# A gated cross-attention and sparse feed-forward kernel: a reordered attention loop, the context's first loads on ScalarE's queue, and moved splits in the feed-forward

## The chip, the core and the metric

The kernel runs on one core of one Trainium2 chip. The metric is the device time of one execution in microseconds (us); less is better. A core has TensorE (PE, with PEld for its weight loads), VectorE (DVE), ScalarE (ACT), GpSimd (POOL) and SyncE (SP), each with its own instruction stream; they meet in semaphores. 16 DMA engines move data between HBM and the on-chip SBUF.

## What is computed

The inputs are x [32, 128, 512], a context of the same shape, a mask [32, 128], two scalar gates and three weights of the feed-forward (512 by 2048 twice, 2048 by 512). `_layernorm` is (x - mean) / sqrt(var + 1e-5). Cut to what matters:

```python
q = _layernorm(x)
scores = einsum('bsd,bmd->bsm', q, ctx) / sqrt(512)
attn = softmax(where(mask[:, None, :], scores, -1e30))
out = einsum('bsm,bmd->bsd', attn, ctx)
out = where(any(mask, -1)[:, None, None], out, 0)
x = x + tanh(g_xattn[0]) * out

n = _layernorm(x)
h = silu(n @ w_gate) * (n @ w_up)
# in each group of 4 neighbours of h the 2 of largest magnitude are kept
x = x + tanh(g_ffn[0]) * (sparsify_2to4(h) @ w_down)
```

## The kernel before

**Attention.** A loop over 39 slots (n from 0 to 38; DVE and POOL start one or two earlier) is software-pipelined over 32 batches of one 128 by 512 tile. Each engine has its own copy of the loop, written out by hand, and in slot n works on several batches at once. On DVE slot n holds two `bn_aggr` (statistics of batch n-6's new row tile and of batch n+1's input; results in `bn_mv`), `neg_scores` and its minimum `neg_max` (batch n-3), `x1`, the attention's output plus x (n-5), `x1n`, that tile normalised (n-6), and two `bn_stats`, of `x1` (n-5) and of `x_in` (n+2). POOL turns variances into powers: `base3` adds eps, `power3` raises to -0.5 (and the softmax sum to -1), `neg_mean` and `neg_mean_rstd` make the bias of `xn`. ACT copies transposed tiles out of PSUM (`ctxT`, `xnT`), makes `probs` (exp), `xn` and `probsT`. PE transposes and multiplies. SP issues the loads, nine batches ahead (INPUTS = 9), and the stores.

**The first weights and activations.** The feed-forward multiplies in float32r with a high and a low part for each operand, and replaces eight block products by seven (PROD = 7) of sums of blocks. Tables by slot place this preparation in the attention loop: `PIECE_AT` (loads of raw weights), `SPREAD_AT` (ACT copies a raw piece into `w_blk`), `SUM_AT` (DVE sums of blocks), `W0_AT` and `X0_AT` (ACT makes the high part, POOL the low part one slot later: `w_ring`, L306, and `xm`, L347; DVE makes the sums of `x_blk` at L354 to L364). A DVE `w_sum` or `x_sum` stands between `neg_max` and `x1`.

**Feed-forward.** 16 steps s of two units u = 2s and 2s+1. A unit is seven products k (two halves e each, 12 matmuls of 128 x 512 per k) followed, from u = 2 on, by the down product of four row tiles (`ps_y`, 48 matmuls). PE starts the first three products in slots 36 to 38. Product 2 waits until ACT has copied product 0 out (`copy_a0`), product 5 for `copy_d0`, a row tile for `copy_y` (`y_out`) of the tile two before it. While weights are built (u < 8) and while the next pair's activations are split (14 points, `x_point(s, point)`), ACT makes `x_high` and DVE `x_low` (L347, `x_out`) and then the next `x_sum`. `dn_low` (L1020) makes the low part of w_down.

What the change and the prediction touch: the start of SP's queue (L421 to L430), the DVE slot (L888 to L943), POOL's slot (L520 to L552), the tables, and the places of `x_high_at`, `x_low_at`, `spread` and `dn_low` in ACT's and DVE's feed-forward code.

Of the kernel before, what the change touches and what calls it, by code (L numbers as in the profile page):

```python
# [5 lines left out]
F32 = mybir.dt.float32  # L6
# [24 lines left out]
BIG = 1e30  # L31
RING = 8
# [15 lines left out]
CONVERT = {1: (0,), 2: (1,), 3: (2, 3)}  # L48
# [6 lines left out]
PIECE_AT = {4: (0, 2), 7: (0, 3), 10: (1, 0), 13: (1, 1), 21: (1, 2), 24: (1, 3), 27: (2, 0), 30: (2, 1)}  # L55
SPREAD_AT = {3: (0, 0), 6: (0, 1), 9: (0, 2), 12: (0, 3), 20: (1, 0), 23: (1, 1), 26: (1, 2), 29: (1, 3)}
SUM_AT = {13: ((0, 0), (0, 1)), 14: ((0, 2),), 15: ((0, 3),), 30: ((1, 0), (1, 1))}
W0_AT = {5: 0, 8: 1, 14: 2, 15: 3, 16: 4, 17: 5, 18: 6}
X0_AT = {19 + i: (0, i) for i in range(7)} | {29 + i: (1, i) for i in range(7)}
# [41 lines left out]
def flamingo_gated(nc, x, ctx, mask, g_xattn, g_ffn, w_gate, w_up, w_down, out):  # L101
# [9 lines left out]
    with whole:  # L111
# [36 lines left out]
        neg_scores = sb("neg_scores", [P, 2, M], F32, 4)  # L148
# [9 lines left out]
        bn_mv = sb("bn_mv", [P, RING, 2, 2], F32, 4)  # L158
# [5 lines left out]
        eps = sb("eps", [P, 2], F32, 4)  # L164
# [3 lines left out]
        valid = sb("valid", [P, B], F32, 4)  # L168
        gate_valid = sb("gate_valid", [P, B], F32, 4)
        ident = sb("ident", [P, P], F32, 4)  # L170
        x_blk1 = sb("x_blk1", [P, 4, HALF], F32, 4)
        mask_in = x1nT[:, 0, 0:2].rearrange("p c n -> p (c n)").bitcast(U8)

# [202 lines left out]
        def _(sp):  # L376
            def load(b):
# [3 lines left out]
                sp.dma_start(ctx_in[:, b % INPUTS], ctx[b]).then_inc(ctx_in_loaded[b % INPUTS], 16)  # L381
# [38 lines left out]

            for b in range(INPUTS):  # L421
                load(b)
                if b == 1:
                    sp.dma_start(mask_in, mask.rearrange("b m -> (b m)").rearrange("(a n) -> a n", a=1)
                                 .to_broadcast([P, B * M])).then_inc(mask_loaded, 16)
# [3 lines left out]
            load_w_piece(sp, nc.sync, 0, 0)  # L429
            load_w_piece(sp, nc.sync, 0, 1)  # L430
# [162 lines left out]
        def _(act):  # L593
# [5 lines left out]
            for n in range(SLOTS):  # L599
# [736 lines left out]
```

## Time and profile before

| | |
|---|---|
| median of 3 runs | 1119.65 us (1117.45 to 1120.14) |
| the profiled execution: its own time | 1116.94 us |
| its span (first to last instruction) | 1115.1 us |
| PE / DVE / ACT / POOL busy, share of the span | 97% / 73% / 56% / 19% |
| granted TensorE clock, mean | 0.998 |
| attention ends, first feed-forward product begins | 134.58 us |

Times in the trace are us from the start of the span. A row of the timeline is start, duration, engine, line, operation, tile written and tiles read, shapes, and, in brackets, how long the engine had been idle and what released it. SPq is SP's DMA issue; its duration is that of the issue, not of the transfer. Time outside the span is 1.8 us.

### The profile page before, as it was taken

Reading aid. Unit: us, or ns where it says so; the run is one execution under the profiler, and the core shown is the slowest. Engines: PE = TensorE matmul, PEld = TensorE weight load, DVE = VectorE, ACT = ScalarE, POOL = GpSimd, SP = SyncE. Lnnn points to the kernel's source line nnn. Section 1 sums busy time; section 2 is a strip of 40 time slices with the busy share of each in tenths; the row PEclk is TensorE's granted clock in tenths of the full one; section 3 lists DMA queues with packets and bytes.
Section 4 is the critical chain, followed back from the end, with each engine's and each line's share of the span. In section 5 each row is a group of like instructions: output and inputs, shape, how many; then the busy total and the mean of one; then the engine's idle time right before and its main releaser. Section 6 shows DMA issues by size and latency. Waiting matters only on the chain.

```text
span 1115.1 us, 15146 instructions
## 1 busy us (share of the span) xinstructions
PE 1082.4 (97%) x4960; PEld 880.0 (79%) x4960; DVE 809.6 (73%) x1400; ACT 620.1 (56%) x1132; POOL 210.6 (19%) x328
## 2 busy tenths in 40 slices
PE   6998799999999999999999999999999999999998
PEld 5776587777878888888888888888888888888886
DVE  6999969879897757576775767675757565565765
ACT  5999678566765544454544444454445454443452
POOL 5576610121210111111111111001111111111111
PEclk9999999999999999999999999999999999999999
DMA  7899586798869977797779777888878666767726
GB/s 273 295 349 329 202 326 226 219 289 280 257 226 354 356 196 198 187 257 185 202 197 374 182 202 200 237 235 208 231 230 274 151 153 156 189 159 189 199 29 137
DMA packets 89533, 254.75 MB, mean 228 GB/s; under 512 B 9072, under 2 KB 9072, under 8 KB 85104
## 3 DMA queue, kind: packets, MB, share of 16 engines
q1 hardware_dynamic: 67856, 205.55, 52.2%
q0 software_dynamic: 21600, 48.24, 26.1%
q8 instruction: 40, 0.66, 0.2%
q14 instruction: 37, 0.30, 0.1%
HBM read 154.14 MB, written 99.61 MB: 228 GB/s over the span
## 4 chain that ended last, share of the span: by engine, by line
PE 73%; DVE 14%; ACT 4%; issue 4%; POOL 2%; DMA 2%; SPq 0%; DVEq 0%; ACTq 0%; POOLq 0%
PE ps_y L1302 9%; PE ps_a L1231 9%; PE ps_a L1233 9%; PE ps_a L1235 9%; PE ps_y L1304 9%; PE ps_y L1303 9%; PE ps_d L1233 4%; PE ps_d L1231 4%; PE ps_d L1235 4%; PE ps_c L1233 2%; PE ps_c L1231 2%; PE ps_c L1235 2%; DVE beats L980 2%; DMA w_raw<-in_L_ffn_w_up 1%; DVE x1n L930 1%
## 5 line engine op out<-in xcount | busy, mean ns | idle before, releaser
L569 POOL DMA_DIRECT2D out_rows<-y_out x124 | 107.1, 871 | 735.2 <-ACT y_out L717 712.7
L1231 PE MATMUL ps_a<-xm,w_ring 128*128 128x512 f32 x512 | 200.7, 392 | 3.6 <-ACT cp L597 3.3
L1233 PE MATMUL ps_a<-xm,w_ring 128*128 128x512 f32 x512 | 200.3, 391 | 0.0
L1235 PE MATMUL ps_a<-xm,w_ring 128*128 128x512 f32 x512 | 200.2, 391 | 0.0
L1302 PE MATMUL ps_y<-dn,h_hi 128*128 128x512 f32 x480 | 188.9, 394 | 4.4 <-ACT y_out L717 3.3
L1304 PE MATMUL ps_y<-dn,h_lo 128*128 128x512 f32 x480 | 187.4, 390 | 0.0
L1303 PE MATMUL ps_y<-dn,h_hi 128*128 128x512 f32 x480 | 187.0, 390 | 0.0
L717 ACT ACTIVATE y_out<-ps_y,ffn_gate 128x512 f32<-128x512 f32 x124 | 84.8, 686 | 158.4 <-PE ps_y L1304 158.3
L694 ACT ACTIVATE h_hi<-hidden 128x512 fp32r<-128x512 f32 x128 | 73.6, 626 | 107.0 <-DVE hidden L1006 107.0
L980 DVE TENSOR_TENSOR beats<-h_abs 128x512 bf16<-128x512 f32 x186 | 117.7, 684 | 1.3 <-ACT h_abs L687 1.3
L1231 PEld LDWEIGHTS ps_a<-xm,w_ring 128*128 128x128 f32 x512 | 96.4, 188 | 26.2 <-issue 5.2
L1235 PEld LDWEIGHTS ps_a<-xm,w_ring 128*128 128x128 f32 x512 | 96.5, 188 | 20.4
L1233 PEld LDWEIGHTS ps_a<-xm,w_ring 128*128 128x128 f32 x512 | 96.4, 188 | 20.0
L1302 PEld LDWEIGHTS ps_y<-dn,h_hi 128*128 128x128 f32 x480 | 90.1, 188 | 27.4 <-ACT y_out L717 7.4
L948 DVE TENSOR_TENSOR cp<-ps_c,cp 128x512 f32<-128x512 f32 x64 | 43.6, 689 | 93.7 <-PE ps_c L1235 93.7
L1304 PEld LDWEIGHTS ps_y<-dn,h_lo 128*128 128x128 f32 x480 | 90.1, 188 | 19.4
L1303 PEld LDWEIGHTS ps_y<-dn,h_hi 128*128 128x128 f32 x480 | 90.2, 188 | 18.7
L1231 PE MATMUL ps_d<-xm,w_ring 128*128 128x512 f32 x256 | 99.7, 390 | 0.5 <-ACT hidden L670 0.5
L1235 PE MATMUL ps_d<-xm,w_ring 128*128 128x512 f32 x256 | 99.6, 389 | 0.0
L1233 PE MATMUL ps_d<-xm,w_ring 128*128 128x512 f32 x256 | 99.6, 389 | 0.0
L954 DVE TENSOR_TENSOR hidden<-ps_a,hidden 128x512 f32<-128x512 f32 x64 | 43.8, 690 | 65.2 <-PE ps_a L1235 62.9
L687 ACT ACTIVATE h_abs<-hidden 128x512 f32<-128x512 f32 x124 | 74.1, 625 | 28.3 <-DVE hidden L972 28.3
(109 smaller groups left out, 1876.6 us busy)
## 6 DMA issues: line engine op xcount, KB each, us to landing
w_ring<-w_scratch SPq DMA_DIRECT2D x147, 512.0 KB, 4.5
out_rows<-y_out POOLq DMA_DIRECT2D x124, 256.0 KB, 4.3
w_scratch<-w_ring SPq DMA_DIRECT2D x56, 512.0 KB, 4.7
xm_scratch<-x_out SPq DMA_DIRECT2D x42, 512.0 KB, 5.4
xm<-xm_scratch SPq DMA_DIRECT2D x21, 1024.0 KB, 8.4
w_raw<-in_L_ffn_w_down SPq DMA_DIRECT2D x9, 1024.0 KB, 7.8
x_in<-in_x SPq DMA_DIRECT2D x32, 256.0 KB, 4.7
ctx_in<-in_ctx SPq DMA_DIRECT2D x32, 256.0 KB, 5.0
```

The lines of the kernel that those rows point to most:

```text
L569: nc.gpsimd.dma_start(out[RING * (n // (2 * TILES * QS)) + TILES * ORDER[order] + n % TILES], y_out[:, n % 4], accum_op=ALU.add).then_inc( ...
L687: nc.scalar.activation(abs_of(s, order)[:, j], hidden[:, h, j], ACT.Abs).then_inc(abs_done, 1)
L694: nc.scalar.activation(h_hi[:, h, j], hidden[:, h, j], ACT.Copy).then_inc(h_hi_done, 1)
L717: nc.scalar.activation(y_out[:, n % 4], ps_y[n % 2][:], ACT.Identity, scale=ffn_gate[:]).then_inc(y_copied, 1)
L954: nc.vector.tensor_tensor(hidden[:, 1, j], ps_a[e][:], hidden[:, 1, j], ALU.add).then_inc(c22_done[e], 1)
L980: nc.vector.tensor_tensor(beats[:, PAIR[i, j]], abs_of(s, order)[:, i], abs_of(s, order)[:, j], ALU.is_ge).then_inc(beats_done, 1)
L1231: nc.tensor.matmul(to, w_ring[:, k, e, 0, c], xm[:, k, 0, c], start=begins and c == 0, stop=False, skip_group_check=not begins)
L1233: nc.tensor.matmul(to, w_ring[:, k, e, 0, c], xm[:, k, 1, c], start=False, stop=False, skip_group_check=not begins)
L1235: last = nc.tensor.matmul(to, w_ring[:, k, e, 1, c], xm[:, k, 0, c], start=False, stop=c == 1, skip_group_check=not begins)
L1302: nc.tensor.matmul(to, h_hi[:, h, j, at], right[:, 0, j], start=at_j == 0, stop=False)
L1303: nc.tensor.matmul(to, h_hi[:, h, j, at], right[:, 1, j], start=False, stop=False)
L1304: last = nc.tensor.matmul(to, h_lo[:, h, j, at], right[:, 0, j], start=False, stop=at_j == GROUP - 1)
```

## The change

- **Context loads.** ACT issues the loads of `ctx_in` 0 to 8 before its loop; SP issues the others.
- **Mask.** One load of 128 x 4096 bytes becomes four of 128 x 1024, and the four reductions `valid` and the product `gate_valid` go. `neg_scores` gets a 129th column of 0.9e30, so that a fully masked batch has all its probabilities 0; `LEAST` keeps the sum of them above 0.
- **POOL.** The softmax sum now lies in `stats` (formerly `bn_mv`) with the variances; one `base3` add covers all and so waits for `probs` too. `neg_mean` moves ahead of `power3`.
- **DVE slot.** `bn_stats` of `x_in` moves from the slot's end to just behind `x1`, ahead of `x1n`. `x_sum` is made in the slot of `X0_AT`, formerly one slot earlier.
- **Tables.** Weight pieces 2 and 3 are loaded, spread and summed earlier, sums one in a slot; the second half of the first pair's activations is split in slots 26 to 32, formerly 29 to 35.
- **Feed-forward.** `x_high_at(s, 3)` and `x_low_at(s, 3)` move into the next step, `x_high_at(s, 1)` behind the next `copy_a0`, `spread(u + 1, 2)` behind `silu1`, `dn_low` ahead of two compares.

```diff
-CONVERT = {1: (0,), 2: (1,), 3: (2, 3)}
+CONVERT = {1: 0, 5: 1, 7: 2, 10: 3}
-W0_AT = {5: 0, 8: 1, 14: 2, 15: 3, 16: 4, 17: 5, 18: 6}
-X0_AT = {19 + i: (0, i) for i in range(7)} | {29 + i: (1, i) for i in range(7)}
+W0_AT = {5: 0, 8: 1, 12: 2, 13: 3, 14: 4, 15: 5, 16: 6}
+X0_AT = {19 + i: (0, i) for i in range(7)} | {26 + i: (1, i) for i in range(7)}
...
         def _(sp):
             def load(b):
...
-                sp.dma_start(ctx_in[:, b % INPUTS], ctx[b]).then_inc(ctx_in_loaded[b % INPUTS], 16)
+                if b >= INPUTS:
+                    sp.dma_start(ctx_in[:, b % INPUTS], ctx[b]).then_inc(ctx_in_loaded[b % INPUTS], 16)
...
             for b in range(INPUTS):
                 load(b)
...
+                if b == 5:
+                    load_w_piece(sp, nc.sync, 0, 0)
+                    load_w_piece(sp, nc.sync, 0, 1)
+                if b == 7:
+                    load_mask(1)
+                if b == 2:
+                    load_mask(0)
...
         def _(pool):
...
                 if third:
                     pool.wait_ge(probs_done, n - 3)
-                part_p = slice(0 if first else 1, 3 if third else 2 if second else 1)
+                nc.gpsimd.tensor_tensor(base3[:, k, part_p], stats[:, k, part_p, 1], least[:, part_p],
+                                        ALU.add).then_inc(base_done, 1)
+                if first:
+                    nc.gpsimd.tensor_tensor(neg_mean[:, k:k + 1], stats[:, k, 0, 0:1], minus_one[:],
+                                            ALU.mult).then_inc(neg_mean_done, 1)
+                pool.wait_ge(base_done, n + 2)
                 nc.gpsimd.tensor_tensor(power3[:, k, part_p], base3[:, k, part_p], exponent3[:, part_p],
                                         ALU.pow).then_inc(power_done, 1)
...
         def _(act):
...
+            for b in range(INPUTS):
+                act.dma_start(ctx_in[:, b], ctx[b]).then_inc(ctx_in_loaded[b], 16)
             for n in range(SLOTS):
...
                     absolute(s - 1, 1, 1)
                     copy_a0(u, 1)
+                    x_high_at(s - 1, 3)
...
-                    x_high_at(s, 1)
...
                     w_high(act, 2, 6)
-                    x_high_at(0, 3)
                     continue
...
                 copy_a0(u, 1)
+                x_high_at(s, 1)
...
                     w_high(act, u + 1, 0)
-                    spread(act, u + 1, 2)
                 silu1(u, 0)
                 silu1(u, 1)
                 if building:
+                    spread(act, u + 1, 2)
                     w_high(act, u + 1, 1)
                     spread(act, u + 1, 3)
...
         def _(dve):
...
-                    dve.wait_ge(mask_loaded, 16)
-                    for m in CONVERT[n]:
-                        nc.vector.tensor_reduce(valid[:, m * RING:(m + 1) * RING],
...
                 if s > 1:
                     add_c11(u, 0)
                     add_c11(u, 1)
+                    x_low_at(s - 1, 3)
...
-                    x_low_at(s, 0)
                     add_c22(u, 0)
                     add_c22(u, 1)
-                    compare(s - 1, 1, REST[2:])
                     if s - 1 in DN_BUILT:
                         dn_low(s - 1)
+                    x_low_at(s, 0)
+                    compare(s - 1, 1, REST[2:])
...
                 elif s == 1:
                     for j in tiles:
                         h_low(0, 0, j)
+                    x_low_at(0, 3)
```

The order of DVE's instructions in one slot with a sum, before (slot 22; names as in the text above, `x_65` is `x1`, `bn_68` the raw statistics):

```order
L892 BN_AGGR bn_mv<-bn_68 128x2
L896 BN_AGGR bn_mv<-bn_68 128x2
L909 SCALAR_TENSOR_TENSOR neg_scores<-ps_c,mask_neg 128x128
L912 TENSOR_REDUCE neg_max<-neg_scores 128x1
L357 TENSOR_TENSOR x_blk<-x_blk 128x512
L924 SCALAR_TENSOR_TENSOR x_65<-ps_y,power_71,x_in 128x512
L930 TENSOR_SCALAR x1n<-x_65,bn_mv,power_71 128x512
L935 BN_STATS bn_68<-x_65 128x6
L943 BN_STATS bn_68<-x_in 128x6
```

and in the changed kernel such a slot on DVE reads:

```order
L903 BN_AGGR stats<-bn_68 128x2
L907 BN_AGGR stats<-bn_68 128x2
L914 SCALAR_TENSOR_TENSOR neg_scores<-ps_c,mask_neg 128x128
L919 TENSOR_REDUCE neg_max<-neg_scores 128x1
L361 TENSOR_TENSOR x_blk<-x_blk 128x512
L930 SCALAR_TENSOR_TENSOR x_65<-ps_y,power_71,x_in 128x512
L935 BN_STATS bn_68<-x_in 128x6
L940 TENSOR_SCALAR x1n<-x_65,stats,power_71 128x512
L945 BN_STATS bn_68<-x_65 128x6
```

The statistics of `x_in` have moved from behind the other two to ahead of `x1n`.

DVE in the first step with a down product (s = 1, unit 2), before; `hidden` is what is kept, `beats` a compare:

```order
L1006 SCALAR_TENSOR_TENSOR hidden<-part,hidden 128x512
L347 TENSOR_TENSOR x_out<-x_blk,x_out 128x512
L357 TENSOR_TENSOR x_blk<-x_blk 128x512
L1013 TENSOR_TENSOR h_lo<-hidden,h_hi 128x512 x4
```

and in the changed kernel at the same place on DVE:

```order
L1008 SCALAR_TENSOR_TENSOR hidden<-part,hidden 128x512
L1015 TENSOR_TENSOR h_lo<-hidden,h_hi 128x512 x4
L351 TENSOR_TENSOR x_out<-x_blk,x_out 128x512
L361 TENSOR_TENSOR x_blk<-x_blk 128x512
L982 TENSOR_TENSOR beats<-h_abs 128x512 x2
```

The low part of the activations and the sum behind it now follow the four `h_lo`.

## Rows read from the trace of the kernel before

**Rows 1.** The stretch behind the build, by windows: length, busy time (instructions).
```profile
340.00:1080.00 740.00, 740.00 (x3253) 609.69 (x3252) 490.20 (x802) 356.22 (x617) 83.89 (x98) 1.00 0.78 213
```

**Rows 2.** Timeline of the start, ACT, DVE; and SP's line L381.
```profile
0.72 1.28 ACT L617 ACT_TABLE_LOAD   x1 [0.72 <-PEq L1326]
5.89 0.81 ACT L617 ACTIVATE xn<-x_in,neg_mean_rstd,power 128x512 f32<-128x512 f32 x1 [3.88 <-POOL neg_mean_rstd L542]
10.48 0.69 DVE L943 BATCH_NORM_STATS2 bn<-x_in 128x6 f32<-128x512 f32 x1 [3.37 <-DMA x_in<-in_x]
15.15 2.31 DVE L900 TENSOR_REDUCE valid<-x1nT 128x8 f32<-128x1024 uint8 x2
26.33 0.75 DVE L924 SCALAR_TENSOR_TENSOR x<-ps_y,power,x_in 128x512 f32<-128x512 f32 x1 [0.26 <-PE ps_y L1272]
...
L381 SPq DMA_DIRECT2D ctx_in<-in_ctx x32: 418/450/1503, 1.2 to 105.4; - x32
```

**Rows 3.** Timeline of one attention slot without a low part on POOL.
```profile
35.11 0.17 DVE L892 BATCH_NORM_AGGREGATE bn_mv<-bn 128x2 f32<-128x6 f32 x1
35.77 0.85 POOL L535 TENSOR_TENSOR power<-base,exponent 128x3 f32<-128x3 f32 x1
36.72 0.55 DVE L930 TENSOR_SCALAR x1n<-x,bn_mv,power 128x512 f32<-128x512 f32 x1
38.38 0.17 DVE L892 BATCH_NORM_AGGREGATE bn_mv<-bn 128x2 f32<-128x6 f32 x1
```

**Rows 4.** Timeline of slot 21, with a sum and a low part.
```profile
78.60 0.16 DVE L892 BATCH_NORM_AGGREGATE bn_mv<-bn 128x2 f32<-128x6 f32 x1
79.32 0.68 DVE L354 TENSOR_TENSOR x_blk<-x_blk 128x512 f32<-128x512 f32 x1
79.92 0.75 DVE L924 SCALAR_TENSOR_TENSOR x<-ps_y,power,x_in 128x512 f32<-128x512 f32 x1
80.07 0.19 POOL L538 TENSOR_TENSOR neg_mean<-bn_mv,minus_one 128x1 f32<-128x1 f32 x1
80.48 1.27 POOL L347 TENSOR_TENSOR xm<-x_blk,xm 128x512 fp32r<-128x512 f32 x1
80.58 1.45 DVE L930 TENSOR_SCALAR x1n<-x,bn_mv,power 128x512 f32<-128x512 f32 x1
83.15 0.16 DVE L892 BATCH_NORM_AGGREGATE bn_mv<-bn 128x2 f32<-128x6 f32 x1
```

**Rows 5.** Timeline of slot 20, with a low part and no sum.
```profile
76.94 0.55 DVE L930 TENSOR_SCALAR x1n<-x,bn_mv,power 128x512 f32<-128x512 f32 x1
77.49 1.27 POOL L347 TENSOR_TENSOR xm<-x_blk,xm 128x512 fp32r<-128x512 f32 x1
```

**Rows 6.** Timeline of slots 34 and 35, the end of attention.
```profile
127.99 0.18 DVE L892 BATCH_NORM_AGGREGATE bn_mv<-bn 128x2 f32<-128x6 f32 x1
132.70 1.41 DVE L930 TENSOR_SCALAR x1n<-x,bn_mv,power 128x512 f32<-128x512 f32 x1 [0.46 <-POOL power L535]
```

**Rows 7.** Timeline of the first pair: TensorE's waits and what stands ahead.
```profile
181.27 0.47 PE L1231 MATMUL ps_a<-xm,w_ring 128*128 128x512 f32 x1 [1.91 <-ACT cp L597]
190.64 0.63 ACT L342 ACTIVATE x_out<-x_blk 128x512 fp32r<-128x512 f32 x1 [0.57 <-DVE x_blk L357]
192.04 0.47 PE L1231 MATMUL ps_d<-xm,w_ring 128*128 128x512 f32 x1 [0.54 <-ACT hidden L670]
...
216.32 0.47 PE L1231 MATMUL ps_a<-xm,w_ring 128*128 128x512 f32 x1 [1.35 <-ACT cp L597]
...
231.02 1.12 ACT L290 ACTIVATE w_blk<-w_raw 128x512 f32<-128x512 f32 x1 [5.04 <-DMA w_raw<-in_L_ffn_w_up]
237.51 0.50 PE L1302 MATMUL ps_y<-dn,h_hi 128*128 128x512 f32 x1 [1.84 <-ACT y_out L717]
...
294.60 0.69 DVE L972 TENSOR_TENSOR hidden<-hidden,cp 128x512 f32<-128x512 f32 x1 [2.03 <-ACT cp L678]
324.93 0.50 PE L1302 MATMUL ps_y<-dn,h_hi 128*128 128x512 f32 x1 [1.09 <-DVE dn L1020]
```

More of the change, by code:

```diff
@@ L31 @@
 BIG = 1e30
+FEW = 0.9e30
+LEAST = 1e-30
 RING = 8
@@ L163, in flamingo_gated @@
         neg_mean_rstd = sb("neg_mean_rstd", [P, RING], F32, 4)
-        eps = sb("eps", [P, 2], F32, 4)
+        least = sb("least", [P, 3], F32, 4)
         minus_one = sb("minus_one", [P, 1], F32, 4)
@@ L526, in _ @@
                     pool.wait_ge(stats2_done, n - 5)
-                if first or second:
-                    part_v = slice(0 if first else 1, 2 if second else 1)
-                    nc.gpsimd.tensor_tensor(base3[:, k, part_v], bn_mv[:, k, part_v, 1], eps[:, part_v],
-                                            ALU.add).then_inc(base_done, 1)
-                    pool.wait_ge(base_done, n + 2)
+                part_p = slice(0 if first else 1, 3 if third else 2 if second else 1)
                 if third:
                     pool.wait_ge(probs_done, n - 3)
-                part_p = slice(0 if first else 1, 3 if third else 2 if second else 1)
+                nc.gpsimd.tensor_tensor(base3[:, k, part_p], stats[:, k, part_p, 1], least[:, part_p],
[4 more added lines that the diff above has]
+                pool.wait_ge(base_done, n + 2)
                 nc.gpsimd.tensor_tensor(power3[:, k, part_p], base3[:, k, part_p], exponent3[:, part_p],
@@ L544, in _ @@
                 if n in CONVERT:
[L545 to L549 removed]
+                    m = CONVERT[n]
+                    pool.wait_ge(mask_loaded[m], 16)
+                    part_m = slice(m * GROUP_M, (m + 1) * GROUP_M)
+                    nc.gpsimd.tensor_scalar(mask_neg[:, part_m], mask_in[:, part_m], -BIG, BIG, ALU.mult,
+                                            ALU.add).then_inc(mask_neg_done, 1)
                 if n - 1 in W0_AT:
@@ L610, in _ @@
                     wait(act, pT_done, b - 1)
-                    nc.scalar.activation(probs[:, b % 2], neg_scores[:, b % 2], ACT.Exp, bias=neg_max[:, b % RING:b % RING + 1],
-                                         scale=-1.0, accum_out=base3[:, (b + 4) % RING, 2:3]).then_inc(probs_done, 1)
+                    nc.scalar.activation(probs[:, b % 2], neg_scores[:, b % 2, 0:M], ACT.Exp, bias=neg_max[:, b % RING:b % RING + 1],
+                                         scale=-1.0, accum_out=stats[:, (b + 4) % RING, 2, 1:2]).then_inc(probs_done, 1)
                 b = n
@@ L914, in _ @@
                 if n in SUM_AT:
-                    for u, i in SUM_AT[n]:
-                        w_sum(dve, u, i)
-                if n + 1 in X0_AT:
-                    x_sum(dve, 0, *X0_AT[n + 1])
+                    w_sum(dve, *SUM_AT[n])
+                if n in X0_AT:
+                    x_sum(dve, 0, *X0_AT[n])
                 b = n - 5
@@ L925, in _ @@
                                                    x_in[:, b % INPUTS], ALU.mult, ALU.add).then_inc(x1_done, 1)
+                b = n + 2
+                if b < B:
+                    dve.wait_ge(x_in_loaded[b % INPUTS], 16 * (b // INPUTS + 1))
+                    nc.vector.bn_stats(bn6[:, 0, b % 2], x_in[:, b % INPUTS]).then_inc(bn1_done, 1)
                 b = n - 6
```

95 lines of the change are left out of this document (37 added, 58 removed).

## The prediction, made before the changed kernel was run

> **What bounds the kernel now.** I read the windows first. From 340 us on TensorE is busy for the whole of each window, 740 of 740 us, while VectorE has a third of its time free [rows 1]. Nothing that the change does there can gain, and it adds no work to TensorE. What can gain is the attention phase (to 134.6 us) and TensorE's waits while weights are built (135 to 340 us). Second, the timeline of the start. VectorE sits 3.37 us until the third x tile lands, then makes the four mask reductions, and ScalarE has its first work only at 5.89 us [rows 2]. Third, the timeline of single slots: VectorE goes from one slot into the next with hardly an idle gap, so that the length of its slot sets the pace [rows 3 to 5]. Fourth, the list of TensorE's waits in the first pair [rows 7].
>
> **The slot of VectorE, which carries the sum.** A slot without a low part on GpSimd takes 38.38 - 35.11 = 3.27 us [rows 3]. In it x1n starts 1.61 us after the slot's first row, though VectorE could reach it at 1.38 (1.98 in slot 21 [rows 4], less 0.60 for the sum ahead of it: 79.92 - 79.32). It waits for power, 35.77 + 0.85 = 36.62. The change puts bn_stats of x_in (0.60: x1n and two of them take 38.38 - 36.72 = 1.66, and x1n 0.46) into this gap: minus 0.23. But the slot's first bn_aggr now reads what the instruction just ahead of it made; I add 0.10 for the 0.69 of its full length in place of the 0.60 from start to start. New free slot: 3.27 - 0.23 + 0.10 = about 3.15.
>
> A slot with a low part is another matter. In slot 20 x1n starts at 76.94 and the low part follows at 77.49, just when x1n ends [rows 5]. In slot 21 the low part starts first, at 80.48, and x1n, issued at 80.58, takes 1.45 in place of 0.55: it ends at 82.03, which is 0.28 behind the end of the low part, 80.48 + 1.27 = 81.75 [rows 4]. The slot is 83.15 - 78.60 = 4.55 long. So whoever starts first makes the other wait. Measured from the slot's first row the low part starts at 1.88 and x1n at 1.98 with a sum; without one x1n came first. After the change x1n starts 0.60 later in each slot, at 1.98 without a sum and 2.58 with one. The low part starts a little earlier than 1.88, since neg_mean (80.07, between power and the low part) goes ahead of power; I take 1.74. It wins in every slot. The new slot is 1.74 + 1.27 + 0.28 = 3.29 to the end of x1n, minus 0.08 of overlap, plus 0.71 for the last bn_stats: 3.92, with or without a sum, against 3.27 and 4.55.
>
> The Trainium skill says the same of the mechanism and speaks against the change (SBUF — State Buffer, "SBUF: two separate sides"): VectorE and GpSimd share a port pair, an exclusive lock for the whole instruction, and the one that starts first gets it. By this rule the trace agrees (1.45 against 0.55).
>
> **Attention, term by term.** I count from x1 in slot 6 to x1n in slot 35, which releases TensorE's transposition and the first product. Before: 132.70 - 26.33 = 106.4 us. After: low parts lie in slots 6, 9, 13 to 17 and 20 to 30, 18 slots, and I count the mask conversions in slots 7 and 10 like them: 20 x 3.92 = 78.4. Slots 8, 18 and 19 are free: 3 x 3.15 = 9.5. Slots 11 and 12 have a sum alone: 2 x 3.75 = 7.5. Slots 31 to 33, which have no bn_stats of x_in any more, stay at the 3.4 of now (slot 34 too: 132.70 - 127.99, less 1.33 to x1n [rows 6]), 10.2. Slots 34 and 35 up to x1n took 132.70 - 127.99 = 4.7 with low parts [rows 6]; without them power, 0.5 behind the slot's first row and 0.8 long, sets about 1.3 in each and x1n and bn_stats follow: 3.8. Sum 109.4, less 0.72, at which x1 stands in its slot (79.92 - 78.60 less the sum's 0.60): 108.7, that is 2.3 slower. In this sum the low parts of 30 to 36 that now end in slot 33, and the stall and double sums of slot 13, are already gained; the collisions take more than all of it. At the end x1n itself has no collision and takes 0.55, not 1.41 [rows 6]: minus 0.9.
>
> **The start.** The third x tile no longer stands behind the whole mask and three context tiles: its 3.37 us go. The reductions go from VectorE, 2 x 2.31 = 4.6 us for four. But ScalarE must first issue nine loads. No row shows a load issued by ScalarE. SP's take 0.42 at least, 1.50 at most [rows 2]. From below: 0.73 + 9 x 0.42 + 1.28 for the table load (which now stands behind them) = 5.8, no later than now. From above: 0.73 + 9 x 1.50 + 1.28 = 15.5. I take 0.6 each, nearer the lower end, as SP's median is 0.45, with something for the second queue that fills beside it; so 7.4, 1.5 late. Then each slot is a round through ScalarE and TensorE, some 2.6 us at first, 3.3 with probs, and about 3.5 in slots 3 and 4, each of which now holds a spread. I get xn of slot 4 at about 19.5 and x1 of slot 6 some 3.6 behind it, 23.1 to 23.3, where 26.33 stands now: minus 3.2. The rest of the 8.0 us removed is lost to that round.
>
> The Trainium skill's DMA page (DMA: Bandwidth & Descriptors, "Issuing engines are not separate DMA queues") says that issuing from several engines only saves issue time. No run here shows more; it would leave the bytes' time as it is.
>
> Attention together: 2.3 - 0.9 - 3.2 = -1.8 us.
>
> **The first pair.** (1) The wait of 1.91 at 181.27 goes: ScalarE stood at x_high of point 3, behind VectorE's sum, and the copy behind it was late; the copy now comes first. (2) What is late next: ScalarE's x_high of step 1 waits for the sum of that same point (190.64 [rows 7]), which VectorE now makes behind four h_lo, 4 x 0.60 = 2.4 us later. Behind it in ScalarE's queue stand the two copy_d0, for which product 5 waits. It starts 2.4 later, at 192.04 + 2.4 = 194.4 (times of before). TensorE, there at 192.04 - 0.54 - 1.91 = 189.6, waits 4.8 in place of 0.54. (3) The wait of 1.35 at 216.32 absorbs most of this: 4.8 against 1.91 + 0.54 + 1.35 = 3.8. Net +1.0 at most. (4) At 237.51 the chain hangs on a weight piece that lands at 231.02; with x_high(1, 1) out of the way ScalarE frees its buffer some 0.9 earlier: net -0.9 there, as TensorE waits 1.84 at that place and the +1.0 is absorbed in it. (5) silu1 no longer stands behind the spread that waits for a load, so VectorE's 2.03 at 294.60 shrink, and dn_low comes 1.2 to 2.4 earlier: of the wait of 1.09 at 324.93 and what VectorE, which is full there, holds up beside it I take 1.3, between 0 and the 2.03. Sum: -2.2 us; bounds +0.5 (4 and 5 bring nothing) and -4.
>
> **Sum.** -1.8 - 2.2 = -4.0. The profiled execution took 1116.94, so 1112.9; its time is 2.7 below the median of the three, and from the median it is 1119.65 - 4.0 = 1115.6. That is 0.36% faster, just past the 0.3% (3.4 us) that a measurement of this kernel can tell from no change.
>
> **Rivals.** (A) The low part does not win the race. Speaking for it: the margin without a sum is 1.98 - 1.74 = 0.24 us, and base3 now also waits for probs. Against it: 0.10 was enough in slot 21. Then 11 slots without a sum (6, 13 to 17, 20, 21, 26 to 28) fall to about 3.3, ScalarE's own slot: 11 x 0.6 = 6.6 more, 1109.
>
> (B) Slower than before: ScalarE's nine issues clog. Its queue backs up as SP's did at its worst (1.50). At 1.5 each xn starts at 15.5, 8.1 later than I take: 1115.6 + 8.1 = 1123.7. Equality with before lies at 0.6 + 4.0/9 = 1.04 us per issue. For it: ScalarE does nothing else meanwhile, all later work hangs on it, and it has eight loads queued at its ninth. Against it: SP's median is 0.45. The Trainium skill (Perfetto Trace Analysis, "DMA Instruction — HWDGE (DVE, Sync)") says that a load's descriptors come from a generator that one sequencer locks at a time; no row here has two sequencers at it. By that rule each issue would wait for one of SP's, 2 x 0.45 = 0.9, xn would start at 10.1, and the sum would be 2.7 less, 1118.3.
>
> (C) The first pair gives nothing, or the 4.8 us wait is not absorbed: -1.8 + 0.5 to +2.5, so 1118 to 1120, within 0.3%. For it: VectorE is full in that stretch and each delay moves on.
>
> (D) The loads don't arrive earlier: DMA engines carry the same bytes, and the third x tile lands only when six tiles are through. For it: the volume is unchanged, and the context's share now flows beside x from the first tile on. Then the start keeps 1 of its 3.2: 1117.8.
>
> **How the numbers follow.** Forecast, between -7 and -1.5 us, 0.50; A 0.12; B 0.14; C 0.14; D 0.10. Predicted time 1115.6. The range 1108.5 to 1121.5 takes in A at its foot and B up to 1.3 us an issue. Faster by over 0.3%: A, and 0.44 of the forecast and rest, 0.58; within 0.3% 0.26; slower 0.16.
>
> **What would show it.** ScalarE's first xn between 6 and 9 us; x1 of slot 6 near 23; x1n taking 1.3 to 1.5 us in nearly all of the slots with a low part, and these 3.9 long; the first product near 132.3. In unit 2 one wait of TensorE for copy_d0 of 4 to 5 us where there were two small ones, and no wait before product 2. It is wrong if x1n stays at 0.55 in slots without a sum, if the nine issues take over 9 us, or if TensorE waits anywhere behind 340 us.

## The result and the profile after

The changed kernel takes 1129.06 us (median; 1125.18 to 1132.69) against 1119.65 in the same runs: a ratio of 1.0082, 95% interval 1.0055 to 1.0109. It is slower by about 9 us. The prediction was 1115.6 us, with a range that ended at 1121.5 and 0.16 on slower. The profiled execution took 1129.06 us with a span of 1127.3, so that 1.8 us lie outside the span, as before.

The first view is again the windows: the stretch behind the build, in which TensorE was busy for every one of 740 us [rows 1].

```profile
340.00:1080.00 740.00, 729.14 (x3192) 599.40 (x3191) 480.21 (x785) 346.67 (x604) 83.26 (x97) 1.00 0.77 212
```

TensorE is idle for 10.9 us there, and does 61 matmuls fewer (3192 for 3253). The timeline of TensorE has these waits in it, those of the first pair ahead of them (which answer to [rows 7]; a further one of 0.58 at 268.16, like the 0.58 before, is left out):

```profile
181.63 0.47 PE L1233 MATMUL ps_a<-xm,w_ring 128*128 128x512 f32 x1 [0.77 <-ACT cp L675]
190.37 0.76 PE L1233 MATMUL ps_d<-xm,w_ring 128*128 128x512 f32 x1 [5.78 <-ACT hidden L681]
235.67 0.50 PE L1304 MATMUL ps_y<-dn,h_hi 128*128 128x512 f32 x1 [1.92 <-ACT y_out L728]
329.64 0.50 PE L1304 MATMUL ps_y<-dn,h_hi 128*128 128x512 f32 x1 [1.17 <-ACT y_out L728]
382.58 0.55 PE L1233 MATMUL ps_d<-xm,w_ring 128*128 128x512 f32 x1 [3.59 <-ACT hidden L681]
516.77 0.50 PE L1304 MATMUL ps_y<-dn,h_hi 128*128 128x512 f32 x1 [1.43 <-ACT y_out L728]
578.53 0.50 PE L1304 MATMUL ps_y<-dn,h_hi 128*128 128x512 f32 x1 [1.46 <-ACT y_out L728]
639.43 0.50 PE L1304 MATMUL ps_y<-dn,h_hi 128*128 128x512 f32 x1 [0.59 <-ACT y_out L728]
761.13 0.50 PE L1304 MATMUL ps_y<-dn,h_hi 128*128 128x512 f32 x1 [1.46 <-ACT y_out L728]
823.77 0.50 PE L1304 MATMUL ps_y<-dn,h_hi 128*128 128x512 f32 x1 [2.33 <-ACT y_out L728]
1101.31 0.48 PE L1304 MATMUL ps_y<-dn_last,h_hi 128*128 128x512 f32 x1 [1.09 <-DVE h_lo L1015]
```

The last row, the first of the last down products, stands in both kernels. The kernel before has it, and the row tile that answers to 329.64, here:

```profile
331.30 0.50 PE L1302 MATMUL ps_y<-dn,h_hi 128*128 128x512 f32 x1 [0.59 <-ACT y_out L717]
1089.21 0.47 PE L1302 MATMUL ps_y<-dn_last,h_hi 128*128 128x512 f32 x1 [1.09 <-DVE h_lo L1013]
```

So two numbers say where the time went. I call these two rows the first and the last mark. At the first mark the changed kernel is 331.30 - 329.64 = 1.66 us ahead. From the first to the last mark it takes 771.67 us where the kernel before took 757.91: 13.8 more. I call this stretch the tail; it is the measure of the experiments below. Of the 13.8, 10.9 are the six waits. Another 1.7 are 3.4 us behind the wait at 382.58 in which the granted clock stood at 1.2 GHz (from 382.8 on; before, the clock was at 1.00 for all of this stretch). The last 1.2 I could not place in a single row.

The wait at 382.58 is read on ScalarE: `x_high` stands 7.13 us for x_blk (2.64 before), and `copy_d0` (L681), which TensorE needs, stands behind it. SP shows why x_blk is late:

```profile
344.01 1.09 SPq L392 DMA_DIRECT2D xm_scratch<-x_out  x1
350.48 4.40 SPq L423 DMA_DIRECT2D xm<-xm_scratch  x7
354.99 0.58 SPq L283 DMA_DIRECT2D x_blk<-xnT_scratch  x1
381.32 0.63 ACT L346 ACTIVATE x_out<-x_blk 128x512 fp32r<-128x512 f32 x1 [7.13 <-DMA x_blk<-xnT_scratch]
381.86 1.06 ACT L681 ACTIVATE hidden<-ps_d 128x512 f32<-128x512 f32 x2
```

The seven loads of xm read what the stores of x_out have written, so SP waits for the last store to land: issued at 344.01, it leaves a hole of 5.3 us in SP's queue. Before, the hole was 0.5 us. The load of x_blk itself is not issued late: 354.99 here and 356.57 before. What the hole costs is the time of the DMA engines, which have little to do in it, so that the 7 MB of xm, and x_blk behind them, are carried later. x_blk takes 26.3 us from issue to landing where it took 21.9. The windows of the changed kernel (the last two numbers are the share of the DMA engines and GB/s):

```profile
348.00:350.00 2.00, 2.00 (x11) 1.65 (x10) 1.07 (x2) 0.00 (x0) 0.00 (x0) 1.00 0.46 169
350.00:352.00 2.00, 2.00 (x10) 1.68 (x9) 0.92 (x2) 0.63 (x1) 0.00 (x0) 1.00 0.43 70
```

and of the kernel before:

```profile
348.00:350.00 2.00, 2.00 (x10) 1.68 (x9) 0.74 (x2) 0.58 (x1) 0.00 (x0) 1.00 1.03 416
350.00:352.00 2.00, 2.00 (x10) 1.65 (x10) 0.72 (x2) 0.00 (x0) 0.00 (x0) 1.00 1.03 356
```

The waits for y_out have another origin. In the list of waits, `dn_high` on ScalarE now waits for the down weights:

```profile
ACT dn L718 <- DMA w_raw<-in_L_ffn_w_down: 11.4, 4, 3.2
```

that is 11.4 us in 4 waits, none of which was there before. The load stands on SP directly behind a store of x_out and is issued at 498.25, where the kernel before issued it at 489.73. The store waits for the low part that the change moved into the next step (`x_out`, 496.91 to 497.59; it was made at 488.39):

```profile
497.62 0.53 SPq L392 DMA_DIRECT2D xm_scratch<-x_out  x1
498.25 0.55 SPq L415 DMA_DIRECT2D w_raw<-in_L_ffn_w_down  x1
```

In the attention phase the timeline shows the start (it answers to [rows 2]) and the slots ([rows 3 to 6]):

```profile
0.72 5.60 ACTq L610 DMA_DIRECT2D ctx_in<-in_ctx  x9
7.65 0.81 ACT L629 ACTIVATE xn<-x_in,neg_mean_rstd,power 128x512 f32<-128x512 f32 x1
12.57 0.69 DVE L935 BATCH_NORM_STATS2 bn<-x_in 128x6 f32<-128x512 f32 x1 [4.25 <-DMA x_in<-in_x]
22.86 0.74 DVE L930 SCALAR_TENSOR_TENSOR x<-ps_y,power,x_in 128x512 f32<-128x512 f32 x1
48.34 1.27 POOL L310 TENSOR_TENSOR w_ring<-w_blk,w_ring 128x512 fp32r<-128x512 f32 x1
48.50 1.40 DVE L940 TENSOR_SCALAR x1n<-x,stats,power 128x512 f32<-128x512 f32 x1
52.46 1.39 DVE L940 TENSOR_SCALAR x1n<-x,stats,power 128x512 f32<-128x512 f32 x1
82.55 1.27 POOL L351 TENSOR_TENSOR xm<-x_blk,xm 128x512 fp32r<-128x512 f32 x1
83.33 0.77 DVE L940 TENSOR_SCALAR x1n<-x,stats,power 128x512 f32<-128x512 f32 x1
129.65 0.55 DVE L940 TENSOR_SCALAR x1n<-x,stats,power 128x512 f32<-128x512 f32 x1 [0.47 <-POOL power L547]
130.66 0.48 PE L1233 MATMUL ps_a<-xm,w_ring 128*128 128x512 f32 x1
```

The row at 129.65 is x1n of the batch that [rows 6] show at 132.70: it starts 3.05 us earlier, and takes 0.55 in place of 1.41. The last row is the first feed-forward product, which stood at 134.58: attention ends 3.92 us earlier. A low part on GpSimd and x1n end 0.28 or 0.29 us apart both without a sum (49.61 and 49.90) and with one (83.82 and 84.10).

### The profile page after: what moved, and what is told of

Read it like the earlier page. It is cut to its first block, busy times and chain, and to the rows that moved or that the text cites. A ratio compares the mean times of both kernels' runs of the same rounds, so it can differ in the third digit from the quotient of the medians.

```text
span 1127.3 us, 15122 instructions
## 1 busy us (share of the span) xinstructions
PE 1084.2 (96%) x4960; PEld 880.3 (78%) x4960; DVE 806.8 (72%) x1395; ACT 617.2 (55%) x1132; POOL 205.9 (18%) x330
## 4 chain that ended last, share of the span: by engine, by line
PE 67%; DVE 16%; DMA 7%; ACT 5%; issue 4%; ACTq 1%; SPq 0%; POOL 0%; DVEq 0%
PE ps_y L1304 8%; PE ps_y L1306 8%; PE ps_y L1305 8%; PE ps_a L1233 8%; PE ps_a L1237 8%; PE ps_a L1235 8%; PE ps_d L1233 4%; PE ps_d L1235 4%; PE ps_d L1237 4%; DMA w_raw<-in_L_ffn_w_down 2%; DMA x_blk<-xnT_scratch 2%; PE ps_c L1237 2%; PE ps_c L1233 2%; PE ps_c L1235 2%; DVE x1n L940 2%
## 5 line engine op out<-in xcount | busy, mean ns | idle before, releaser
L1304 PE MATMUL ps_y<-dn,h_hi 128*128 128x512 f32 x480 | 189.0, 394 | 10.9 <-ACT y_out L728 10.9
L1233 PE MATMUL ps_d<-xm,w_ring 128*128 128x512 f32 x256 | 101.3, 396 | 9.4 <-ACT hidden L681 9.4
L1235 PE MATMUL ps_d<-xm,w_ring 128*128 128x512 f32 x256 | 101.2, 395 | 0.0
L1237 PE MATMUL ps_d<-xm,w_ring 128*128 128x512 f32 x256 | 101.0, 394 | 0.0
```

Source lines behind the costliest of these rows:

```text
L1233: nc.tensor.matmul(to, w_ring[:, k, e, 0, c], xm[:, k, 0, c], start=begins and c == 0, stop=False, skip_group_check=not begins)
L1235: nc.tensor.matmul(to, w_ring[:, k, e, 0, c], xm[:, k, 1, c], start=False, stop=False, skip_group_check=not begins)
L1237: last = nc.tensor.matmul(to, w_ring[:, k, e, 1, c], xm[:, k, 0, c], start=False, stop=c == 1, skip_group_check=not begins)
L1304: nc.tensor.matmul(to, h_hi[:, h, j, at], right[:, 0, j], start=at_j == 0, stop=False)
```

## The experiments

The programs, and for each the start of the first mark, the length of the tail, the time of the profiled execution from which these two are read, and the median of all executions. The kernel before was timed again beside runs 1 to 4, 5 to 8 and 9 to 12; its median there was 1118.41, 1118.99 and 1119.28, so ratios are the better comparison. A mark comes from one execution, which can lie up to 2.7 us above or below its median (the kernel before is 2.7 below, run 5 is 1.7 above, run 10 is 1.2 below, run 8 is 2.5 above).

| kernel | first mark | tail | profiled | median | ratio to before (95%) |
|---|---|---|---|---|---|
| before | 331.30 | 757.91 | 1116.94 | 1119.65 | |
| changed | 329.64 | 771.67 | 1129.06 | 1129.06 | 1.0082 (1.0055 to 1.0109) |
| 1 attention alone | 330.39 | 757.92 | 1116.03 | 1116.08 | 0.9971 (0.9960 to 0.9982) |
| 2 feed-forward alone | 331.40 | 769.63 | 1128.73 | 1130.89 | 1.0109 (1.0092 to 1.0127) |
| 3 three mends | 327.13 | 764.63 | 1119.50 | 1119.66 | 1.0011 (1.0000 to 1.0023) |
| 4 down weights first | 327.62 | 766.88 | 1122.25 | 1123.22 | 1.0044 (1.0027 to 1.0061) |
| 5 four mends | 328.29 | 759.23 | 1115.25 | 1113.51 | 0.9948 (0.9935 to 0.9961) |
| 6 five mends | 327.10 | 760.52 | 1115.36 | 1114.70 | 0.9959 (0.9947 to 0.9971) |
| 7 attention, context on SP | 327.15 | 760.03 | 1115.28 | 1114.75 | 0.9962 (0.9950 to 0.9974) |
| 8 before, one store moved | 336.62 | 764.87 | 1129.25 | 1126.76 | 1.0071 (1.0059 to 1.0084) |
| 9 attention, statistics last | 328.78 | 758.02 | 1114.54 | 1114.60 | 0.9965 (0.9952 to 0.9978) |
| 10 four mends, context on SP | 325.67 | 758.38 | 1112.11 | 1113.27 | 0.9957 (0.9943 to 0.9971) |
| 11 with x_blk first | 326.43 | 760.40 | 1114.97 | 1114.89 | 0.9963 (0.9950 to 0.9975) |
| 12 and statistics last | 327.85 | 760.64 | 1116.61 | 1114.66 | 0.9964 (0.9952 to 0.9977) |

**1 and 2. Which half of the change loses?** The change is two edits that hardly touch. The first run takes the tables, the loads, the mask and the attention slots of the changed kernel and the feed-forward code of the kernel before; the second the reverse.

> The kernel before with the new attention alone (its tables, the context's loads on ScalarE's queue, the mask in four pieces, the third power); the feed-forward section of all three queues is that of before. Theory A (the loss is made by the feed-forward's moved points): TensorE has no wait between 340 and 1080 us, x1n of batch 29 starts about 3.0 us earlier than the 132.70 of before, and of that 1.5 to 3 us reach the end: 1116.7 to 1118.2 us against 1119.65. Rival B (the new attention brings the loss, since everything that follows starts earlier while the transfers of scratch tensors do not): waits of together about 10 us stand behind 340 us here too, and the time is about 1129 us.

> The kernel before with only the feed-forward's moves: x_high and x_low of points 1 and 3 one unit later, the spread behind silu1, compare(REST[2:]) and x_low_at(s, 0) behind dn_low. Theory A: the waits behind 340 us are those of the changed kernel (about 10.8 us in six places, plus 2 to 3 us at a lower granted clock), so the time is 1130 to 1133 us. Rival B: none of them, 1118 to 1120 us.

Attention alone gains 0.29% and has a tail of 757.92 us, to a hundredth that of before. The feed-forward's moves alone lose 1.1%. Their waits are nearly those of the changed kernel (one more of 0.80 at 395.97, and a smaller one at 761.00); the list of TensorE's waits of the second run from 340 to 1090 us says:

```profile
PE ps_y L1298 <- ACT y_out L714: 7.0, 6, 2.3
PE ps_d L1227 <- ACT hidden L667: 3.2, 1, 3.2
```

Rival B is dead. The two ratios add up to the whole: -0.29% and +1.09% are +0.80%, measured +0.82%.

**3 and 4. Which of the moves?** Three places suggested themselves: the down weights behind a store on SP's queue; `x_low_at(s, 0)`, now behind `add_c22` on VectorE; and point 1, now in the unit after. Run 4 has the first edit alone, run 3 all three:

```diff
-                        x_stored_at(s, 2 * half + 1)
                         if half == 1 and s >= QS and s in DN_BUILT and s != LAST:
                             load_dn(s)
+                        x_stored_at(s, 2 * half + 1)
...
                     compare(s - 1, 1, first + second + REST[:2])
+                    x_low_at(s, 0)
                     add_c22(u, 0)
                     add_c22(u, 1)
+                    compare(s - 1, 1, REST[2:])
                     if s - 1 in DN_BUILT:
                         dn_low(s - 1)
-                    x_low_at(s, 0)
-                    compare(s - 1, 1, REST[2:])
...
```

The third edit puts `x_high_at(s, 1)` and `x_low_at(s, 1)` back at the end of unit 2s for the last step of a pair.

> The changed kernel with load_dn(s) ahead of x_stored_at(s, 3) on SP's queue, nothing else. Theory A: w_down is issued 8 us earlier, ScalarE's four waits for it (11.4 us) go, and the waits for y_out at 516.77, 578.53, 761.13 and 823.77 fall from 1.43, 1.46, 1.46 and 2.33 to about 0.6 each (what x_low behind add_c22 costs); the one at 382.58 stays. 4 us less than the changed kernel: 1124 to 1126 us. Rival C: no change of those waits, 1129 us.

> The changed kernel with three small edits, one for each group of its waits: load_dn(s) issued ahead of x_stored_at(s, 3); x_low_at(s, 0) ahead of add_c22 and compare(REST[2:]) ahead of dn_low as before; point 1 of the last step of a pair (s % 4 == 3) back at the end of unit 2s. Theory A with these three causes: the waits at 382.58 (3.59 us), at the five y_out (7.3 us) and the clock's share after them (2 to 3 us) go, 11 to 14 us less than the changed kernel: 1115 to 1118 us. Rival C (the late w_down and x_blk come from DMA traffic that is heavier in the changed kernel, not from the place in SP's queue): the waits of y_out shrink only by the 0.6 us each of x_low, together 3 us: about 1126 us.

In run 4 ScalarE has no wait for w_down left, and the waits for y_out shrink, but only to these two sizes (three of the first, two of the second):

```profile
512.41 0.50 PE L1304 MATMUL ps_y<-dn,h_hi 128*128 128x512 f32 x1 [0.57 <-ACT y_out L728]
573.86 0.50 PE L1304 MATMUL ps_y<-dn,h_hi 128*128 128x512 f32 x1 [1.17 <-ACT y_out L728]
```

The place in SP's queue was the cause of what went, 0.0082 - 0.0044 of 1119.65, 4.3 us, and not heavier traffic (rival C). The intervals of the two ratios overlap a little (1.0055 to 1.0061); the tails differ by 4.8 us. At 1123.22 us it is a little under the 1124 to 1126 expected. Run 3 removes what was left of these five as well: 0.57 us is what the one `x_low` takes, at 0.6 from start to start, that the change put between `add_c22` and the first y_out, and 1.17 is an `x_low` with the sum behind it (564.82 and 565.43 in run 4). Ahead of `add_c22` they filled time in which VectorE waited for TensorE; behind it that VectorE chain has no slack, so 0.6 us in it is 0.6 us of TensorE.

But half of the expectation of run 3 fell. It came out at 1119.66 us, not 1115 to 1118, because the large wait stayed although point 1 was back in its old unit:

```profile
380.13 0.77 PE L1243 MATMUL ps_d<-xm,w_ring 128*128 128x512 f32 x1 [3.64 <-ACT hidden L685]
```

and the list of SP's waits still has the hole, 4.4 us:

```profile
SPq L426 <- DMA xm_scratch<-x_out: 4.4, 1, 4.4
```

The instructions of VectorE and ScalarE were those of before at this place; SP's were not.

**5 and 8. One store on SP's queue.** The change had also made two branches into one:

```diff
 for k in range(4):
     store_w(u + 1, k)
-if half == 0:
-    x_stored_at(s, 1)
 for k in range(4, PROD):
     store_w(u + 1, k)
-if half == 1:
-    x_stored_at(s, 3)
+x_stored_at(s, 2 * half + 1)
```

Run 5 puts that store back for the one step where the loads of xm follow (s = 3); run 8 makes this edit alone in the kernel before, as the change did, in all three steps that have it (s = 1 to 3).

> The three mends, and on SP's queue in the last step of the first pair x_stored_at(s, 1) again between the fourth and fifth store_w, where it stood before. With the three mends TensorE still waited 3.63 us at 380.13 for copy_d0 behind x_high, which waited 7.2 us for x_blk; SP waited 4.4 us for the landing of that store before it issued the seven loads of xm, with the DMA engines idle. Theory D (the rank of one store on SP's queue makes x_blk late): SP's wait for xm_scratch falls to about 0.5 us, the wait of 3.63 goes and the granted clock does not halve behind it (6.8 us at half rate, 3.4 us), so 5 to 7 us less: 1113 to 1115 us, 2 us under attention alone. Rival E (x_blk is late since the whole kernel is now ahead of its transfers, DMA being busy all of that time): the wait stays at 2 us or more, 1118 to 1119 us.

> The kernel before with one move on SP's queue: x_stored_at(s, 1) behind store_w(u + 1, 4..6) instead of ahead of them, no instruction of another engine moved. Theory D: in step 3 the seven loads of xm and the load of x_blk wait for the landing of that store, 4 to 5 us in place of 0.5, TensorE gets a wait of 3 to 4 us near 380 us where there was none, and the time is 3.5 to 7 us above before: 1122 to 1126 us. Rival E: no wait there, the time of before.

Both say the same. The timeline of run 5 has the store at 339.10, with the weight stores behind it, and TensorE's wait of 3.64 is 0.30 (in the list of waits the hole is 0.7 us):

```profile
339.10 0.52 SPq L396 DMA_DIRECT2D xm_scratch<-x_out  x1
377.94 0.47 PE L1246 MATMUL ps_d<-xm,w_ring 128*128 128x512 f32 x1 [0.30 <-ACT hidden L688]
```

The timeline of run 8 has the weight stores first and the store last, and a wait of 3.98 appears in a kernel that had none (the hole is 3.7 us):

```profile
352.16 1.24 SPq L387 DMA_DIRECT2D xm_scratch<-x_out  x1
390.00 0.76 PE L1228 MATMUL ps_d<-xm,w_ring 128*128 128x512 f32 x1 [3.98 <-ACT hidden L667]
```

This one move costs 7.9 us in the kernel before (0.71%, at 1126.76 just above the 1122 to 1126 expected) and gives 7.0 back in the mended one (0.63%), against 3.6 to 4.0 us of visible wait. Part of the cost is thus not in the wait itself; run 8's tail is 6.96 us longer. In run 8 the granted clock stood at 1.2 GHz from 389.3 to 396.2, that is for 6.2 us behind the end of the wait, which is 3.1 us of work lost against 2.4 GHz; run 5 shows 2.4 GHz throughout there. Wait and clock give 7.1, which covers the 6.96. Run 8's profiled execution, its slowest, is also 5.3 us late at the first mark already, 3.3 of it in longer waits (3.60 at 239.80 where 1.84 stood). That wait hangs on a load of a weight piece, and run 1, which has the store in its old place, has 3.55 there; so nothing shows that the store caused it, and I rest on the tail and the medians.

With 1113.51 us run 5 beats both kernels. It keeps the change's attention and its first pair, and was 2.3 points of a thousand below attention alone.

**6. The predicted wait at 190 us.** On VectorE, `x_low_at(0, 3)` goes ahead of the four `h_lo` of step 1.

> The four mends, and x_low_at(0, 3) ahead of the four h_lo at the head of step 1 on VectorE, nothing else. The wait of 5.74 us at 190.35 (copy_d0 behind x_high, which waits for the sum of that point) falls by the 2.4 us of four h_lo to about 3.3, so 2.4 us less than the four mends, and up to 1.7 more if one of the two half-rate stretches behind that wait goes. Rival F (VectorE is full there and h_lo is late instead): TensorE waits for h_lo or y_out by as much, no change.

The wait falls from 5.78 to 3.51, by 2.3 for four `h_lo` of 0.60. Half of it is gone 45 us later, where TensorE waits 2.58 for y_out where it waited 1.21; at the first mark run 6 is still 1.2 us ahead of run 5. The rest goes in 1.59 of waiting for copy_d0 at 378.04 (0.30 in run 5): at the last mark the two are level, 1087.62 and 1087.52.

```profile
188.69 0.47 PE L1246 MATMUL ps_d<-xm,w_ring 128*128 128x512 f32 x1 [3.51 <-ACT hidden L688]
231.61 1.11 ACT L298 ACTIVATE w_blk<-w_raw 128x512 f32<-128x512 f32 x1 [3.43 <-DMA w_raw<-in_L_ffn_w_up]
234.38 0.80 PE L1317 MATMUL ps_y<-dn,h_hi 128*128 128x512 f32 x1 [2.58 <-ACT y_out L735]
```

The middle row is what holds the wait for y_out: ScalarE stands 3.43 us for a weight piece to land. Rival F had the amount right and the releaser, a load, wrong.

**7. The context's loads.** Attention alone, with the nine loads on SP again, each behind its x.

> The new attention alone (as in the first run) with the nine first loads of the context on SP's queue again, each behind its x. Theory G (the loads on ScalarE's queue are what lets x arrive in time): the first xn starts near 5.9 instead of 7.8 us but the later x tiles land later, and x1 of slot 6 comes 1 to 2 us later than 22.9: 1117 to 1118 us. Rival H (the start is bound by the round through ScalarE and TensorE, the nine issues cost what they give): within 0.5 us of attention alone. Rival I: it is faster by the 1.5 us by which the first xn comes sooner, 1114.5 us.

x1 of the first batch is at 18.89 us here and at 20.30 in run 1, and x1n of batch 29 at 128.23 against 130.04. So issuing them on ScalarE costs 1.8 us of attention. In the whole time the intervals overlap (0.9962 and 0.9971): in the profile, run 7 is 3.2 us ahead of run 1 at the first mark, and a wait of 1.62 us at 378.12 takes half of it, for copy_d0, which stands behind an `x_high` that waited 5.16 us for x_blk. Theory G is refuted, H and I are not told apart by the time.

**9. VectorE's order.** Attention alone, `bn_stats` of x_in at the slot's end again.

> The new attention alone, with bn_stats of x_in at the end of VectorE's slot again, behind bn_stats of x1. Theory J (as predicted: that instruction ahead of x1n makes x1n meet the low part on GpSimd): in the slots with a low part and no sum (48.72 to 64.53, 102, 106, 114) x1n takes 0.55 instead of 1.40 and these slots shrink from 3.95 to about 3.4, so that x1n of batch 29 starts 3 to 5 us earlier than the 130.04 of attention alone, at 125 to 127. Rival K (ScalarE's own slot or GpSimd's sets the pace there): x1n is short but the slots stay at 3.8 or more, 129 to 130. To the whole time both add little, 1113.5 to 1116 us, if x_blk's landing near 377 holds TensorE.

```profile
49.96 0.55 DVE L940 TENSOR_SCALAR x1n<-x,stats,power 128x512 f32<-128x512 f32 x1 [0.17 <-POOL power L550]
53.25 0.55 DVE L940 TENSOR_SCALAR x1n<-x,stats,power 128x512 f32<-128x512 f32 x1 [0.16 <-POOL power L550]
81.44 1.37 DVE L940 TENSOR_SCALAR x1n<-x,stats,power 128x512 f32<-128x512 f32 x1
85.92 1.37 DVE L940 TENSOR_SCALAR x1n<-x,stats,power 128x512 f32<-128x512 f32 x1
```

Slots with a low part and no sum do shrink, from 3.96 to 3.29 us, as theory J says. But those with a sum grow from 3.96 to 4.48, and x1n of batch 29 is at 129.94 against 130.04. Here the order decided which slots collide, and the sum of what is lost stayed the same. J's 3 to 5 us were wrong, and so was K's reason, though its number was right.

**10, 11 and 12. Is there a floor at x_blk?** In runs 5, 6 and 7 TensorE went on at 377.94, 378.04 and 378.12, though it had come there at 377.64, 376.45 and 376.50.

> The four mends with the context's first loads on SP's queue. The start is 1.8 us earlier. Theory L (x_blk lands near 377 whatever is gained ahead of it, since the DMA engines are full from 340 us on): TensorE waits 1.5 to 2.3 us for copy_d0 near 376 and goes on at 378, the time is that of the four mends alone, 1113 to 1114 us. Rival M (the gain passes through): no wait there over 0.5 us, 1111.5 to 1112 us.

> The four mends, the context's loads on SP, and load_x_blk of the next pair issued ahead of the seven loads of xm instead of behind them. Theory L: x_blk lands by 360, ScalarE's wait of 3.8 to 5.2 us for it goes, TensorE has no wait for copy_d0, and 1.5 to 3 us are gained against the run before it: 1110.5 to 1112.5 us. Rival N (the xm loads, later by one megabyte, 2.5 us, become the wait): TensorE waits for xm instead, 1113 to 1115 us.

> The run before it with bn_stats of x_in at the end of VectorE's slot again. Theory J: attention ends 3 to 5 us earlier and, with x_blk early, most of it reaches the end: 1107 to 1109.5 us. Rival K: no change in attention, 1110.5 to 1112.5 us.

Run 10's profile has no wait there: x_blk has landed by 372.9, where ScalarE had it at 376.7 in run 5, so its landing is no fixed floor. It reaches the last mark at 1084.05, 3.5 us ahead of run 5; but the medians differ by 0.2 us only. The two profiled executions explain most of this: run 5's, at 1115.25, was its slowest, and run 10's, at 1112.11, was 1.2 below its median. By the medians M's gain (1111.5 to 1112) is not there, so the 1.8 us of the start are not shown to reach the end. Run 11 did away with ScalarE's wait for x_blk, and another load was late in its place:

```profile
378.93 1.68 ACT L723 ACTIVATE dn<-dn_raw 128x512 fp32r<-128x512 f32 x3 [5.21 <-DMA dn_raw<-in_L_ffn_w_down]
382.15 0.50 PE L1315 MATMUL ps_y<-dn,h_hi 128*128 128x512 f32 x1 [0.90 <-DVE dn L1030]
```

The DMA engines are busy for 0.95 of the window from 331 to 392 us in run 11 as in the kernel before; putting one load first there only made another one the last. Run 11's 1114.89 lies in rival N's range, but the late load was the down weights' and not xm. Run 12, at 1114.66, added nothing; J's and K's ranges both lay below it. Neither beats run 5.

## Why the prediction was wrong

**The step that failed** is its first: "Nothing that the change does there can gain", of the stretch behind 340 us, where it then priced nothing. A full TensorE means that nothing can be gained, not that nothing can be lost; all 13.8 us were lost there. Its last paragraph named the sign ("if TensorE waits anywhere behind 340 us") but gave it neither a chance nor a price. Two instances could be read from the program. SP's edit of the store's rank was not mentioned: 7 to 8 us. And of the points moved to the next unit the prediction counted what ScalarE and VectorE do, not the SP waits that follow from them, `load_dn` behind `x_stored_at(s, 3)`: 4.3 us. The third, `x_low` behind `add_c22`, with the move of point 1 in the last step of a pair, is the rest: 0.0044 - 0.0011 of 1119.65, 3.7 us. Together the three and the store give 0.0082 + 0.0052 = 1.34%, 15 us, and the version without them is where a gain was forecast, lower than the forecast even: 1113.5. That it lies so near the forecast is in part luck, since the two terms of the sum missed in opposite directions, as follows.

**The slot.** Right in length and partly in form. 3.92 us was said of a slot with a low part, 3.96 measured (48.50 to 52.46). Without a sum x1n takes 1.39 to 1.41, in the band given; with a sum it takes 0.77, since it starts later against the low part. The time from x1 of slot 6 to the start of x1n of batch 29 was said to grow by 2.3 us and grew from 106.37 to 106.79, 0.4; the 0.9 that x1n itself then saves came out as 0.86. Rival A (the low part loses) is out: in the changed kernel it starts first, 48.34 against 48.50.

This is what the Trainium skill's "SBUF — State Buffer", section "SBUF: two separate sides", states: of a GpSimd operation and a VectorE one of the kinds that it names, the one that starts first holds the shared ports for the whole instruction. By this rule the trace agrees, in the 0.28 us between the two ends in either kind of slot.

**The start.** The forecast was xn at 7.4 and x1 of slot 6 at 23.1 to 23.3; measured 7.65 and 22.86. The nine issues take 5.60 us, 0.62 each against 0.60 taken, so rival B is out. A cause was wrong though: "its 3.37 us go" did not happen. The third tile's wait shrank to about 1 us, but the fourth tile then made VectorE wait 4.25 (at 12.57); in run 7, with the loads on SP, x1 of slot 6 is at 21.53, 4.8 us before the 26.33 of before. That is what the reductions that went, the mask in pieces and the new order give together (no run tells them apart), and the loads on ScalarE take 1.4 of it back. Rival D's mechanism thus holds in part, not its size.

The prediction also gave a figure by the rule of the Trainium skill's "Perfetto Trace Analysis", section "DMA Instruction — HWDGE (DVE, Sync)", a generator that one sequencer locks: xn at 10.1. The page names the sequencers of VectorE and SyncE for it; the prediction carried it over to ScalarE. The trace does not agree with that sum: xn came at 7.65. What is seen is milder, and stands below.

**Attention.** -1.8 forecast, to the first product, which was to stand near 132.3. It stands at 130.66: -3.92, twice the forecast, since the slots grew by 0.4 and not 2.3. In the whole time attention alone gives 3.2 us (run 1).

**The first pair.** The wait of 1.91 at 181.27 for L597 is gone, as said; one of 0.77 for another copy (L675) stands at 181.63. The new wait for copy_d0 was put at 4.8 and is 5.78. The one at 216.32 is gone, absorbed as said. Step (4) was to bring 0.9 more at 237.51. That row came 1.84 us earlier, at 235.67, but 3.92 had been gained ahead of it, so 2.1 were lost on the way. The old first pair loses them too: in run 1 the first product is at 131.06, and the row at 235.68, behind a wait of 3.55. There ScalarE waits until 232.91 for a weight piece to land. From the first product to the first mark the kernel before takes 196.7 us. With the new attention the old first pair takes 198.4 in the mean of runs 1, 7 and 9 (197.8 to 199.3), the new one 197.1 in the mean of the changed kernel and runs 3, 4, 5, 10, 11 and 12 (196.3 to 199.0). So two things were wrong with the -2.2: the new first pair gives about 1.2 us and not 2.2, as far as single executions that scatter by 2.7 us tell, and some 1.6 of what attention gains don't get through the old one, for which the sum had no term. The medians say no more: run 5 against run 1 is 0.9948 to 0.9971, 2.6 us in favour of the new first pair with intervals that just meet, but run 10 against run 7, the same comparison with the context on SP, is 0.9957 to 0.9962, 0.6 us with intervals that overlap.

## What to carry to other kernels

Where one engine is busy all of the time, ask of a change what it can lose there, and go through every queue that it touches, SP's first: a DMA issue has a rank, and a queue in order passes each delay of its head on to loads that have nothing to do with it. Look at the DMA engines too: a hole in the queue is paid for while they stand idle, even where the load that comes late is issued on time. A store whose landing is waited for should be issued as early as it can be, with other issues behind it to cover the trip. And before sizing a gain, look for the next landing that all of it will run into.

## What was not expected of the hardware

**Issuing from two sequencers.** With SP alone an issue takes 0.39 to 0.43 us (run 7's first six). With ScalarE issuing beside it, both begin at 0.4 to 0.45, and from 2.6 us on SP's take more: SP's x loads 3 to 5 take 1.97 us together, ScalarE's nine 5.60. Eighteen issues are through in 5.6 us, about 0.31 us each, where one sequencer at a pitch of 0.47 needs 8.5. So the second one helps, but not twofold.

**What a wait of TensorE costs beyond itself.** Around the waits near 380 us the granted clock was at 1.2 GHz for 3.4 us (3.59 us of waiting in the changed kernel and 2.12 in run 4), for 6.8 us (3.64 in run 3, 3.98 in run 8), or not at all (3.21 in run 2). The 3.4 us lie behind the wait. The 6.8 us begin inside it, 1.5 us before its end in run 3 and 0.7 in run 8, so that 5.3 and 6.2 us of work ran at half rate. So a wait of 3.2 to 4.0 us costs 0, 1.7, 2.7 or 3.1 us of work beyond itself. Two programs that are the same up to there also lost different amounts at the same place: the changed kernel and run 4 have a granted clock of 0.91 and 0.94 in the window 185 to 240.
